# Causal attention batch by batch: the first batch's out-projection and norm placed inside the second batch's units, query tiles in another order

## What is computed

```python
q, k, v = (split_heads(h @ W.T + b) for W, b in ...)   # 32 heads of 16, h = layernorm(x)
scores = q @ k.T / sqrt(16), causal mask (lower triangle)
att = softmax(scores) @ v
x = x + layernorm(att @ Wo.T + bo)
logits = layernorm(x) @ gate_w        # 8 experts, top 2 of each token
```

## Time and profile before

| | us |
|---|---|
| median of 3 runs | 1693.57 (1690.9 to 1695.56) |
| the profiled execution's own time | 1690.58 |
| its span | 1688.6 |
| mean granted TensorE clock | 0.964 |
| PE, DVE, ACT, POOL busy | 1534.2, 1196.5, 806.9, 927.8 |
| first scores of the units | 1227.75 |
| first transposes of the out-projection | 1498.97 |
| logits complete (L1574 starts) | 1552.30 |
| first gather | 1567.72 |

### The profile page before, as it was taken

One profiled execution on the slowest core, in us unless ns is written; L12 is line 12 of the kernel. 1 busy time (PEld: TensorE's weight loads), 2 busy tenths in 40 slices (PEclk: granted clock), 3 DMA queues, 4 the chain that ended last, 5 costly groups with the idle time before them and its releaser, 6 DMA issues.

```text
span 1688.6 us, 26177 instructions
## 1 busy us (share of the span) xinstructions
PE 1534.2 (91%) x8646; PEld 1191.1 (71%) x8646; DVE 1196.5 (71%) x2000; ACT 806.9 (48%) x1604; POOL 927.8 (55%) x953
## 2 busy tenths in 40 slices
PE   5899999999999999999999969997889898986894
PEld 3677877877878778778777757885656666666682
DVE  5778788787788787887787875656656676767423
ACT  3464555555555555545555424332156776662230
POOL 4367576677685775766776851005462334236643
PEclk9999999999999999999999999998889999996897
DMA  3111112021110110110211112121122222321434
GB/s 121 38 50 58 19 51 63 12 81 37 50 62 19 50 62 13 50 64 10 81 38 50 57 51 70 55 101 49 36 52 52 50 56 59 103 118 69 148 126 162
DMA packets 60249, 105.19 MB, mean 62 GB/s; under 512 B 12624, under 2 KB 37328, under 8 KB 54928
## 3 DMA queue, kind: packets, MB, share of 16 engines
q1 hardware_dynamic: 50352, 85.88, 15.9%
q0 software_dynamic: 9824, 18.37, 3.9%
HBM read 81.14 MB, written 10.49 MB: 54 GB/s over the span
## 4 chain that ended last, share of the span: by engine, by line
PE 59%; DVE 16%; POOL 8%; issue 7%; ACT 6%; DMA 3%; SPq 0%; POOLq 0%; DVEq 0%; ACTq 0%
PE banks L366 28%; PE banks L1679 6%; DVE tap L1255 4%; PE banks L1816 3%; PE banks L1935 3%; PE banks L1744 2%; PE banks L1906 2%; PE banks L1709 2%; PE banks L1738 2%; DMA x<-in_w_gate 2%; PE banks L1924 2%; POOL wol L371 2%; DVE nmax L1518 2%; PE banks L1753 2%; DVE xbc L1261 1%
## 5 line engine op out<-in xcount | busy, mean ns | idle before, releaser
L1255 DVE SCALAR_TENSOR_TENSOR tap<-banks,parg,tap 128x511 f32<-128x511 f32 (+2 forms) x288 | 215.2, 747 | 26.7 <-ACT tap L965 19.4
L752 POOL TENSOR_TENSOR am<-ah,upto 128x1024 fp32r<-128x1024 f32 x64 | 121.7, 1902 | 178.3 <-PE banks L1709 137.2
L366 PE MATMUL banks<-xTh,wch 128*128 128x512 f32 x384 | 162.8, 424 | 6.0 <-DVE em L1361 4.5
L973 ACT ACTIVATE th<-tap 128x512 f32<-128x512 f32 x96 | 60.7, 632 | 213.2 <-DVE tap L1255 211.1
L366 PE MATMUL banks<-xTh,wcl 128*128 128x512 f32 x384 | 151.1, 393 | 0.0
L366 PE MATMUL banks<-xTl,wch 128*128 128x512 f32 x384 | 150.4, 392 | 0.0
L1193 ACT ACTIVATE prob<-banks,nmax 128x128 f32<-128x128 f32 (+3 forms) x256 | 121.8, 527 | 53.4 <-DVE nmax L1518 44.7
L1518 DVE TENSOR_REDUCE nmax<-banks 128x2 f32<-128x256 f32 (+3 forms) x128 | 104.9, 819 | 40.4 <-PE banks L1925 40.4
L752 POOL TENSOR_TENSOR am<-al,upto 128x1024 fp32r<-128x1024 f32 x64 | 122.2, 1909 | 0.0
L890 POOL DMA_DIRECT2D kz<-qh x128 | 61.7, 490 | 104.8 <-DVE ql L1498 81.6
L1361 DVE TENSOR_TENSOR em<-banks,gmask 128x1024 f32<-128x1024 f32 x64 | 78.2, 1222 | 50.6 <-ACT banks L1014 49.7
(11 more groups left out here) (286 smaller groups left out, 4271.8 us busy)
## 6 DMA issues: line engine op xcount, KB each, us to landing
x<-grownT SPq DMA_DIRECT2D x96, 128.0 KB, 4.8
x<-in_w_conv SPq DMA_DIRECT2D x7, 1536.0 KB, 6.6
x<-in_w_gate SPq DMA_DIRECT2D x8, 1024.0 KB, 4.9
x<-in_w_out SPq DMA_DIRECT2D x8, 1024.0 KB, 4.8
eraw<-in_expert_w SPq DMA_DIRECT2D x8, 1024.0 KB, 7.8
gur<-in_ff_gu SPq DMA_DIRECT2D x7, 1024.0 KB, 4.8
x<-in_hidden SPq DMA_DIRECT2D x16, 256.0 KB, 3.9
qs<-qh SPq DMA_DIRECT2D x64, 64.0 KB, 2.0
```

Of the source, the lines that this page charges most:

```text
L366: m = nc.tensor.matmul(o, a, b, start=first and n == 0, stop=last and n == len(terms) - 1)
L752: m = pool.tensor_tensor(am[:, part, :, :], a[:, i, :].bitcast(F32).unsqueeze(2).to_broadcast([P, HG, P]), upto[:, :].unsqueeze(1).to_broa ...
L973: nc.scalar.activation(th[:, :], tap[:, q % 2, :], ACT.Tanh).then_inc(tanh_ready, 1)
L1255: nc.vector.scalar_tensor_tensor(tap[:, q % 2, sh:L], bk(CONV_BANKS[q % 2])[:, 0:L - sh], parg[:, KC * q + k:KC * q + k + 1], tap[:, q % 2 ...
```

## The change

1. Quads run batch by batch: b = quad // 8. Projection m is for batch m // 4 and weights m % 4, so each of the 8 projections loads, scales, rounds and splits its own weights; those of m = 1 come ahead of the units.
2. Query tiles in the order 0, 2, 1, 3. Value products part 0 move from step 6 of their quad to step 0 of the next.
3. The k pieces of a projection move from s = 4 to 7 to s = 5 to 8.
4. The out-projection of tiles 0 to 3 (batch 0) runs in bank 7 in the last four blocks: transposes and ACT copy at units 74, 90, 106 and 113, low part one unit on, six matmuls in each of the two units behind that, bias four units on.
5. The norms of these tiles are four DVE steps, two units apart, from units 84, 100, 115 and 120; GpSimd does its part in `early_norm`, behind the DMAs of a quad.
6. On GpSimd the DMAs of a block's first quad now come ahead of the low part of the weights.
7. The stage behind the units holds tiles 4 to 7 only, the turns and logits of tiles 0 to 3 among their products. The first five experts' weights are loaded after the fourth early out-projection (their room covers its buffers).

```diff
-        A_AHEAD, B_AHEAD, O_BACK = 6, 10, 12
+        A_BACK, B_AHEAD, O_BACK = 8, 10, 12
         def unit(n):
-            return n // 8, n % 8 // 2, n % 2
+            return n // 8, (0, 2, 1, 3)[n % 8 // 2], n % 2
...
-            t, b, u = quad // 4, quad // 2 % 2, quad % 2
+            b, t, u = quad // 8, quad // 2 % AT, quad % 2
...
-            for w, at in ((0, (0, 1, 2, 3)), (1, (4, 5, 6, 7))):
+            for w, at in ((0, (0, 1, 2, 3)), (1, (5, 6, 7, 8))):
...
+        def out_step(n):
+            for i, at in enumerate((8 * 8 + 10, 8 * 10 + 10, 8 * 12 + 10, 8 * 14 + 1)):
+                if at <= n < at + 5:
+                    return i, n - at
+            return None, None
+        def norm_step(n):
+            for i, at in enumerate((8 * 10 + 4, 8 * 12 + 4, 8 * 14 + 4 - 1, 8 * 14 + 8)):
+                if n in (at, at + 2, at + 4, at + 6):
+                    return i, (n - at) // 2
+            return None, None
+        TURN_AT = (4, 5, 6, 7, 9, 10, 11, 12)
+        LOGITS_AT = (5, 6, 7, 8, 10, 11, 12, 13)
...
+                sp.wait_ge(ao_ps, CH)
                 for e in EARLY:
                     load_expert(e)
...
+                def early_norm(i):
+                    norm_wait(pool, 3, "var0", i + 1)
+                    pool.tensor_tensor(rs[:, 0, i:i + 1], ve[:, 0, i:i + 1], mhalf[:, 0:1], ALU.pow).then_inc(nsem["rstd0"], 1)
+                    norm_wait(pool, 3, "out", i + 1)
+                    pool.tensor_tensor(x[:, i, :], x[:, i, :], acc[:, i, :], ALU.add).then_inc(nsem["x"], 1)
+                    norm_wait(pool, 3, "var1", i + 1)
+                    pool.tensor_tensor(rs[:, 1, i:i + 1], ve[:, 1, i:i + 1], mhalf[:, 0:1], ALU.pow).then_inc(nsem["rstd1"], 1)
...
                 pool.wait_ge(sel_ready, SEL + 3)
+                weights_low(1)
                 for k in range(KT):
                     pool.wait_ge(aw_hi, KT + k + 1)
                     low(pool, awl[:, k, :], awr[:, k, :], awh[:, k, :]).then_inc(aw_lo, 1)
-
                 padded(1)
                 for m in range(1, AT * NB):
-                    t = m // NB + 1
-                    if m % NB == 1 and t < AT:
-                        for w in range(2):
-                            pool.wait_ge(aq_hi, 2 * t + w + 1)
-                            low(pool, aql[:, w, :, :], aqr[:, w, :, :], aqh[:, w, :, :]).then_inc(aq_lo, 1)
                     pool.wait_ge(qk_l, 2 * m + 2)
-                    for u in range(2):
-                        padded(2 * m + u)
+                    padded(2 * m)
+                    if m + 1 < AT * NB:
+                        weights_low(m + 1)
+                    padded(2 * m + 1)
+                    if m >= AT + 1:
+                        early_norm(m - AT - 1)
+                early_norm(CH - 1)
...
-                        if n % 32 == 9 and n // 32 + 1 < AT:
-                            weights(n // 32 + 1)
+                        if n % 16 == 9 and n // 16 + 2 < AT * NB:
+                            weights(n // 16 + 2)
+                        i, step = out_step(n)
+                        if step == 0:
+                            act.wait_ge(at_ps, i + 1)
+                            at_least(act, ao_ps, i)
+                            nc.scalar.copy(attEh[:, :], bk(7)).then_inc(at_hi, 1)
...
+                    i, step = norm_step(n)
+                    if step == 0:
+                        tile_done(dve, 3, i)
+                        early_moments(0, i, acc[:, i, :])
+                    if step == 1:
+                        norm_wait(dve, 3, "rstd0", i + 1)
+                        nc.vector.tensor_scalar(acc[:, i, :], acc[:, i, :], mv[:, 0, i, 0:1], rs[:, 0, i:i + 1],
+                                                ALU.subtract, ALU.mult).then_inc(nsem["out"], 1)
+                    if step == 2:
+                        norm_wait(dve, 3, "x", i + 1)
+                        early_moments(1, i, x[:, i, :])
+                    if step == 3:
+                        norm_wait(dve, 3, "rstd1", i + 1)
+                        nc.vector.tensor_scalar(acc[:, i, :], x[:, i, :], mv[:, 1, i, 0:1], rs[:, 1, i:i + 1],
+                                                ALU.subtract, ALU.mult).then_inc(nsem["xn"], 1)
...
+                    i, step = out_step(n)
+                    if step == 0:
+                        pe.wait_ge(att_ready, QUADS // 2)
+                        pe.wait_ge(qk_l, 2 * (n // 16) + (4 if n // 16 + 1 < AT * NB else 2))
+                        at_least(pe, ao_ready, i)
+                        for k in range(KT):
+                            m = pe.transpose(bk(7)[:, k * P:(k + 1) * P], att[:, i, k * P:(k + 1) * P], ident[:, :])
+                        m.then_inc(at_ps, 1)
+                    if step in (2, 3):
+                        pe.wait_ge(at_lo, i + 1)
+                        pe.wait_ge(aw_lo, 2 * KT)
+                        m = products(bk(7), [(attEh[:, k * P:(k + 1) * P], attEl[:, k * P:(k + 1) * P], awh[:, k, :], awl[:, k, :])
+                                             for k in (2 * step - 4, 2 * step - 3)], first=step == 2, last=step == 3)
+                        if step == 3:
+                            m.then_inc(ao_ps, 1)
```

More of the change, by code:

```diff
@@ L636, in _, with norm_round @@
             sp.wait_ge(stored, 16 * NT)
-        def norm_round(q, n):
+        def norm_round(q, n, start=0):
             d = norm_steps
@@ L649, in norm_round @@
             i = n - lag
-            if q < STAGES and 0 <= i < NT:
+            if q < STAGES and start <= i < NT:
                 nc.vector.wait_ge(x_in, 16 * NT) if q == 0 else norm_wait(nc.vector, q, "x", i + 1)
@@ L655, in norm_round @@
             i = n - 1
-            if q and 0 <= i < NT:
+            if q and start <= i < NT:
                 norm_wait(nc.vector, q, "rstd0", i + 1)
@@ L694, in norm_vector, with norm_pool @@
                     made += 1
-        def norm_pool(q, n):
+        def norm_pool(q, n, start=0):
             i = n - 1
@@ L1169, in _ @@
                         high(0, i - NT + 2)
+                weights(1)
                 act.wait_ge(v_ps, NT)
@@ L1182, in _ @@
                         act.wait_ge(pt_ps, 2 * w + 1)
-                        if w % 4 == 0 and quad >= 1:
+                        if w % 8 in (0, 2) and quad >= 1:
                             act.wait_ge(pv_ps, 2 * quad - 1 + hf)
@@ L1551, in _ @@
                             lows(m, w)
-                dve.wait_ge(wide_in, 32)
-                for i in range(NT + 1):
+                    i, step = out_step(n)
+                    if step == 1:
+                        dve.wait_ge(at_hi, i + 1)
+                        low(nc.vector, attEl[:, :], bk(7), attEh[:, :]).then_inc(at_lo, 1)
+                    if step == 4:
+                        dve.wait_ge(wide_in, 32)
+                        dve.wait_ge(ao_ps, i + 1)
+                        nc.vector.tensor_tensor(acc[:, i, :], bk(7), abo[:, :], ALU.add).then_inc(ao_ready, 1)
+                    i, step = norm_step(n)
+                    if step == 0:
+                        tile_done(dve, 3, i)
+                        early_moments(0, i, acc[:, i, :])
+                    if step == 1:
+                        norm_wait(dve, 3, "rstd0", i + 1)
[8 more added lines that the diff above has]
+                                                ALU.subtract, ALU.mult).then_inc(nsem["xn"], 1)
+                for i in range(CH, NT + 1):
                     if i < NT:
```

105 lines of the change are left out of this document (60 added, 45 removed).

## The result

The changed kernel took 1695.54 us (median of 20 runs, 1693.2 to 1697.89); the kernel before, beside it on the same chip, 1690.38. The ratio is 1.0036, 95% interval 1.0028 to 1.0043: slower, by 5 to 6 us. The forecast was 1699.5 for a median before of 1693.57, or +5.9; that median came from 3 runs, and the 20 of now lie 3.2 lower, so it is the difference that can be compared. The profiled execution's span is 1692.3 us, against 1688.6 before, at a mean clock of 0.966 against 0.964.

A forecast was written before the change was run, and what follows sets the result against it. The prediction saw TensorE near its limit, with quads bound by a loop over TensorE, VectorE and ScalarE. Its terms summed to +5.9 us, which on the median before of 1693.57 gave 1699.5, range 1685 to 1710.

The forecast's parts named there:

- stage behind the units: Behind the units: with four tiles left instead of eight, the last bias addition comes 14.2 us earlier; ends -16 and -12.
- out-projection in the units: In the last four blocks: four early tiles' products and transposes cost 3.25 us each, +13.0; 10 to 13, up to 16.
- norms in the units: VectorE's moments and subtractions for four early tiles: half is paid, 1.5 us a tile, +6.0; ends nothing and 12.4.
- list of tokens: After the logits: GpSimd's low parts end 5.0 us later and hold three of VectorE's four first steps, +2.9; 0 to 3.9.
- start: Ahead of the units: GpSimd's two extra low parts come before the output weights' four, with nothing covering them, +2.5 us.
- projection pieces: k pieces a unit later: TensorE's wait goes, but the second maximum is delayed; -0.3 in seven blocks, -2.1; ends -6.5 and 0.
- GpSimd's order: Block boundaries: DMAs ahead of the weights' low part remove the late first scores, -3.5 us; ends -4.1 and 0.
- weights for each projection: In the units: ScalarE scales and rounds weights in six blocks, not three; a third is paid, +1.8 us; ends 0 and 5.6.
- order of tiles and products: Quads: both orders within 0.2 us, taken as 0, loss up to 5; -0.5 at the last quad, part 0 in idle time.
- the steps fill idle time: Rival, in the units: the moved steps fit VectorE's idle time and norms cost 0; -9.8, 1683.8 us; chance 0.22.
- GpSimd's queue is late: Rival, block boundaries: early norms delay DMAs of k, 3.5 us at up to three boundaries, +10.5, 1710 us; chance 0.10.
- Half of that: Rival, no change: half the idle-time effect on norms, pieces, weights and list, -1.6; 1692 to 1695 us; chance 0.35.

The follow-up runs named there:

- x1: Changed kernel without its early steps: out-projection, norms and turns of batch 0 back behind the units, the rest of the change kept; 1688.70 us, ratio 0.9988.
- x2: Changed kernel with VectorE's steps of the four early norms on 16 of 512 columns, same instructions and waits; 1690.22 us, ratio 0.9997.
- x5: Changed kernel with the two low parts of the second projection's weights, ahead of the units, on VectorE instead of GpSimd; 1692.18 us, ratio 1.0017.
- x12: Kernel before with only the k pieces moved one unit later (s = 5 to 8); 1683.31 us, ratio 0.9973.
- x8: Kernel before with only the k pieces at s = 5 to 8 and GpSimd's DMAs ahead of the weights' low part; 1680.13 us, ratio 0.9941.
- x9: Changed kernel without early out-projection and norms, in the old order of query tiles with part 0 at step 6 of its quad; 1681.00 us, ratio 0.9968.
- x4: Changed kernel with the k pieces back at s = 4 to 7; 1696.57 us, ratio 1.0032 to the kernel before.
- x3: Changed kernel in the old order of query tiles, with value products part 0 at step 6 of their quad again; 1689.61 us, ratio 0.9993.
- x10: Changed kernel in the old order of query tiles, but value products part 0 left at step 0 of the next quad; 1690.75 us, ratio 1.0016.
- x6: Changed kernel with the last two of GpSimd's low parts of the experts' weights on VectorE, behind the list; 1696.00 us, ratio 1.0039.
- x11: Changed kernel with the old order of tiles and products, and the low-part moves to VectorE of x5 and x6; 1683.27 us, ratio 0.9971.
- x7: Changed kernel with GpSimd's low part of the weights ahead of the next block's DMAs of k again; 1709.89 us, ratio 1.0118.

## Why the number was right, and which of its parts were not

| term | predicted | measured | by |
|---|---|---|---|
| stage behind the units | -14.2 | -14.6 | landmarks |
| out-projection in the units | +13.0 | +12.9 | x1, x2 |
| norms in the units | +6.0 | +5.3 | x1, x2 |
| list of tokens | +2.9 | +3.0 | landmarks |
| start | +2.5 | +2.5 | timeline, x5 |
| projection pieces | -2.1 | -2.8 | x12 |
| GpSimd's order | -3.5 | -6.2 | x12 to x8 |
| weights for each projection, with batch order | +1.8 | +0.2 | x8 to x9 |
| order of tiles and products | 0, -0.5 | +4.6 | x9 to x1 |
| clock in block 5 | none | +1.6 | windows; but see GpSimd's order below |

The terms in the units add up to +15.6 (-2.8 - 6.2 + 0.2 + 4.6 + 12.9 + 5.3 + 1.6), and the two profiles differ by 15.7. Each was measured in the surroundings of its own run, so they would be parted otherwise in another order: in the new order of tiles the move of the pieces is worth nothing (x4). Ahead of the first landmark there are 1.2 more: 2.5 of the start, -0.7 of the pieces in block 0, and -0.6 that was not parted.

**What held.** The early steps are paid for almost in full: TensorE's 3.24 of an out-projection costs 3.18 to 3.29 (2.6 to 2.8 in plain second quads of the old order, x3), and of VectorE's norm about half is on the path, as taken: the moments' steps, not the subtraction between them (x2). The stage behind the units gives back 14.6, by the sum's working, and the list takes 3.0, also by its working: three steps are held, the reduction is not. Here the Trainium skill's rule (SBUF: State Buffer, the section on the two separate sides) gave 2.9 where the row alone allowed 3.9, and the trace agrees with the rule: 0.27 for the reduction beside GpSimd. So moving batch 0's tail into the units loses in either order of tiles. In the old one, x9 to x3, the units grow by 17.6, the stage shrinks by 14.6, the list grows by 3.1: +6.1, and the spans differ by 5.9 (1679.2 and 1685.1).

**The step that failed is the order of tiles.** The prediction had "by hand both orders give quads within 0.2 us" and took 0. It costs 0.8 in each plain second quad, 4.6 over the units, and more with an out-projection in them: 6 to 7 us of the time (x3; its units are 6.9 shorter in the profile, of which 1.6 is the clock's fall in the changed kernel's). The working counted part 0 "ahead of the second scores as it stood ahead of the last ones", as one place for another. They are not alike: in the old order it cost 0.50 ahead of the last scores, and ahead of the second ones, behind the eight transposes of tile 3 and with a projection's piece behind it, it costs 1.00 (x10). The order of the tiles adds 0.36 in such a quad (x1 to x10), which no single wait explains, and what it costs in first quads depends on where the pieces stand: none with late pieces (x1, x9), and with early ones it gains 0.5 there (18.41 in x4 for 18.94 before). My own sign for it, second quads clearly off 13.9, is what the trace shows. The range given for it (a loss up to 5) nearly held it.

**The pieces and GpSimd's order were undersized together.** -5.6 was taken, -9.0 is there (x8), and -0.7 in block 0. The pieces alone give -3.5 of that for -2.1, since of what they gain in six first quads (4.6) they lose 1.8 in the second quads where the DMAs are late; that loss is in truth part of the other term, which is therefore worth 6.2, beyond the end of 4.1 that I gave it. Two edits to one second quad were costed one by one. Part of the 6.2 is clock: in the kernel before, TensorE's wait of 2.29 ahead of block 5 is followed by 3 us at a granted clock of 0.52 (last section), about 1.6 of block 4's 3.48. So the kernel before had its fall of the clock too, the new order of GpSimd's work took it away with the wait, and the changed kernel's fall in block 5 put as much back. And one row was misread: first quads hold 18 of the projection's 24 matmuls, second quads the other 6. Against the last block's quads without any (13.84), the first paid 5.1 for 4.2 of work and the second 0.15 for 1.4. This was the room that the pieces had to gain from.

**Weights for each projection** cost next to nothing: ScalarE's 1.9 in three more blocks gives +0.2 (x8 to x9). That it lies ahead of exponentials that wait for VectorE anyway fits, but was not tested.

In the units the errors are +5.1 (order of tiles), +1.6 (clock), -2.7 (GpSimd's order), -1.6 (weights), -0.7 (pieces), -0.7 (norms) and -0.1: +0.9 together. That was luck; for the changed kernel in the old order of tiles (x3) the same sum would have missed by 6.

**Against the signs given ahead:** blocks 5 and 6 were to be 5 longer than 33.1 (6.6 with the clock's fall, 5.0 without, and 4.0), block 4 as before (36.2), block 7 32 to 33 (32.1), the stage 39 (38.7), the list's steps 1.2 (1.17 to 1.30), the first exponential 2.5 later (2.5). These hold, and so does the sign of an error: second quads off 13.9. Of the rivals, "the steps fill idle time" falls by x1 and x2, "GpSimd's queue is late" by the changed kernel's second quads. "Half of that", a change of -1.6, would be right for the changed kernel in the old order (x3, 0.8 below the kernel before).

**The stage in x1_late.** In the new order x1_late needs 54.9 us from the transposes to the logits where x9_late_old needs 53.3. That is a fall of the clock and not the order: its first twelve products take 4.61 for 3.06, at a granted clock of 0.63 and 0.52 (1496 to 1500) for 1.00.

**Left open.** Why the order of the tiles adds 0.36 to a second quad, and what the 0.6 ahead of the first landmark are. The parts of GpSimd's order and of the pieces were parted in the kernel before alone, not under the new order in both.

## What to carry to other kernels

A step moved from a stage with idle engines into a software-pipelined loop is free only where the loop's own chain has a gap at that very place, and an engine's idle share says nothing of that: here VectorE was idle for 10 of 37 us, and a moments' step between two of its maxima still came out of the end in full as far as it could be shortened (0.51 of 0.51), while shortening a subtraction in the same quad gained next to nothing. An idle stretch of TensorE can cost twice, once as a wait and once as a slower clock behind it. Cost edits that touch the same few steps of such a loop together, since two of them here were worth 9 us and a third took 5 of it back. And when a change bundles several edits, run the small ones alone on the old kernel: the two cheapest lines were the only gain.

## What the runs showed of the hardware

**The clock fell inside the units.** Windows of the changed kernel around the product that took 2.67 us instead of 1.65, and the TensorE row ahead of it:

```profile
1415.00:1422.00 7.00, 5.28 (x51) 3.77 (x53) 4.80 (x11) 4.51 (x11) 1.86 (x4) 1.00 0.23 56
1422.00:1425.00 3.00, 3.00 (x35) 1.59 (x35) 0.96 (x3) 2.46 (x6) 3.00 (x7) 0.58 0.36 66
```

```profile
1421.68 0.33 PE L2013 MATMUL banks<-ident,prob 128*128 128x128 f32 x1 [1.72 <-DVE pB L1582]
```

TensorE had been idle for 1.72 us, waiting for VectorE, and then ran for 3 us at a granted clock of 0.58, so at 1.2 of its 2.4 GHz for most of it. That quad takes 19.70 in the changed kernel and in x6, 18.06 to 18.09 in x2, x4 and x5. In x4 and x5 the fall comes in the last block, where a quad takes 18.9 instead of 17.4 at a window clock of 0.91, and no wait over 1.2 us stands ahead of it in the block; in x10 it is in block 5 (19.18 for 17.58). In x2, x3 and x11 there is none in the units.

The kernel before has such a fall too, in block 4, behind the wait of 2.29:

```profile
1396.00:1399.00 3.00, 3.00 (x13) 2.81 (x13) 1.12 (x2) 1.22 (x3) 3.00 (x8) 0.52 0.53 144
```

Its eight transposes take 1.89 there and, on the row three microseconds later, 1.04, and the whole fall costs about 1.6. From the first value product of part 1 to the last, in all fourteen kernels, TensorE waited 2.08 us or longer six times (once before, once in x12, four times in x7), and each time the clock was down right behind it. It waited 1.71 to 1.85 us fourteen times, twice in each of seven kernels, and the clock fell behind three of these (changed, x6, x10). So a fall of some 1.6 us can come at no fixed place of a profiled execution; what decides it was not settled. Each kernel has one profile, so how often an execution of the same kernel has one is not known either.

**Small operations beside GpSimd.** A cast of 16 elements, and products of 128 and of 64, take 1.27, 1.30 and 1.17 us beside GpSimd's low parts, about one such low part (13.74 / 11 = 1.25) whatever their size, and 0.2 to 0.3 without it (the earlier trace rows for the cast, 0.23 for `chosen` in x6). The reduction takes 0.27 in either.
